# The output biases of three decision trees on TensorE: f32 products over 128 rows, or bf16 products over 32 rows in three exact parts

## What is computed

```python
def _fff(x, node_w, node_b, w1, b1, w2, b2):
    for _ in range(DEPTH):                      # DEPTH = 4
        score = jnp.einsum('nd,nd->n', xf, node_w[cur]) + node_b[cur]
        cur = 2 * cur + 1 + (score >= 0).astype(jnp.int32)
    sel = jax.nn.one_hot(cur - N_NODES, N_LEAVES)
    hidden_all = jax.nn.relu(jnp.einsum('nd,ldh->lnh', xf, w1) + b1[:, None, :])
    hidden = hidden_all * sel.T[:, :, None]
    out = jnp.einsum('lnh,lho->no', hidden, w2) + sel @ b2
q, k, v = _fff(x, *q_weights), _fff(x, *k_weights), _fff(x, *v_weights)
attn = jax.nn.softmax(jnp.einsum('bqd,bkd->bqk', q, k) * scale, axis=-1)
return jnp.einsum('bqk,bkd->bqd', attn, v)
```

## Time and profile before

| what | us |
| --- | --- |
| median of three runs | 1132.84 |
| lowest and highest of the three | 1128.87, 1138.29 |
| span of the profiled execution, first to last instruction | 1131.2 |
| TensorE busy in it | 1003.4 (89%) |
| VectorE busy | 620.1 (55%) |
| ScalarE busy | 533.9 (47%) |
| GpSimd busy | 199.7 (18%) |

### The profile page before, as it was taken

One profiled execution on the slowest core, in us unless ns is written; L12 is line 12 of the kernel. 1 busy time (PEld: TensorE's weight loads), 2 busy tenths in 40 slices (PEclk: granted clock), 3 DMA queues, 4 the chain that ended last, 5 costly groups with the idle time before them and its releaser, 6 DMA issues.

```text
span 1131.2 us, 11557 instructions
## 1 busy us (share of the span) xinstructions
PE 1003.4 (89%) x3694; PEld 435.2 (38%) x3694; DVE 620.1 (55%) x1160; ACT 533.9 (47%) x978; POOL 199.7 (18%) x176
## 2 busy tenths in 40 slices
PE   5799999999799999998877996867778999999896
PEld 2345555454222222332233663322224444444343
DVE  2222323332888878767334435379998544645573
ACT  4232223232367667766732442665665424464540
POOL 9100000000000000000274551256663000000000
PEclk9799999999899999999988997989999999999998
DMA  8630000030011211210012436000000211110032
GB/s 168 203 101 1 1 1 1 1 91 0 22 50 43 71 43 42 61 33 1 6 35 52 121 91 190 6 5 1 0 1 1 94 55 47 46 40 19 5 108 75
DMA packets 67020, 54.70 MB, mean 48 GB/s; under 512 B 18584, under 2 KB 58829, under 8 KB 66868
## 3 DMA queue, kind: packets, MB, share of 16 engines
q1 hardware_dynamic: 64660, 51.26, 16.0%
q0 software_dynamic: 2304, 2.76, 0.8%
HBM read 41.65 MB, written 13.77 MB: 49 GB/s over the span
## 4 chain that ended last, share of the span: by engine, by line
PE 71%; DVE 11%; ACT 6%; issue 6%; POOL 2%; DMA 2%; another core or an unknown queue 1%; DVEq 0%; SPq 0%; POOLq 0%; ACTq 0%
PE psum L692 68%; ACT sb_scr L1654 3%; DVE sb_scr L2338 3%; DVE sb_scr L2687 2%; DVE sb_scr L2696 2%; ACT sb_qstack L1654 1%; ACT psum L1654 1%; PE psum L1265 1%; PE psum L849 1%; POOL sb_qstack L626 1%; PE psum L1247 1%; POOL sb_scr L672 0%; DVE sb_scr L2213 0%; DVE sb_x L2189 0%
## 5 line engine op out<-in xcount | busy, mean ns | idle before, releaser
L1654 ACT ACTIVATE sb_scr<-psum 128x512 f32<-128x512 f32 (+3 forms) x640 | 318.6, 536 | 361.6 <-PE psum L692 305.5
L692 PE MATMUL psum<-sb_h,sb_wide 128*128 128x512 f32 x448 | 210.4, 599 | 0.8 <-ACT sb_scr L1654 0.8
L2338 DVE TENSOR_REDUCE sb_scr<-psum 128x2 f32<-128x1024 f32 x128 | 154.9, 1223 | 46.2 <-PE psum L692 45.5
L692 PE MATMUL psum<-sb_scr,sb_wide 128*128 128x512 f32 x256 | 126.3, 594 | 0.8 <-DVE sb_scr L2742 0.8
L692 PEld LDWEIGHTS psum<-sb_h,sb_wide 128*128 128x128 f32 x448 | 83.5, 193 | 93.1 <-issue 91.4
L692 PE MATMUL psum<-sb_kstack,sb_qstack 96*128 96x512 bf16 x256 | 98.4, 395 | 8.3 <-DVE sb_scr L2338 8.1
L2277 DVE TENSOR_SCALAR sb_scr<-psum,sb_b 128x512 f32<-128x512 f32 x48 | 34.6, 748 | 126.1 <-PE psum L692 126.1
L692 PE MATMUL psum<-sb_qstack,sb_kstack 128*128 128x512 bf16 x256 | 99.3, 394 | 3.9 <-ACT sb_scr L1654 2.8
L672 POOL TENSOR_TENSOR sb_scr<-sb_scr 128x512 f32<-128x512 f32 x64 | 83.0, 1302 | 91.7 <-ACT sb_scr L1654 46.0
L1654 ACT ACTIVATE sb_scr<-psum,sb_b 128x512 f32<-128x512 f32 x48 | 31.2, 684 | 137.1 <-PE psum L692 137.1
L643 POOL COPY sb_wide<-sb_wide 128x512 f32<-128x512 f32 x4 | 2.5, 618 | 511.2 <-ACT sb_scr L1654 511.2
(11 more groups left out here) (274 smaller groups left out, 1291.1 us busy)
## 6 DMA issues: line engine op xcount, KB each, us to landing
sb_scr<-weight_rows SPq DMA_DIRECT2D x32, 256.0 KB
sb_qstack<-q_bounce SPq DMA_DIRECT2D x48, 96.0 KB
sb_kstack<-k_bounce SPq DMA_DIRECT2D x144, 32.0 KB
sb_scr<-pick_rows SPq DMA_DIRECT2D x8, 512.0 KB
expert_in<-sb_scr SPq DMA_DIRECT2D x4, 645.0 KB, 6.5
sb_scr<-expert_in SPq DMA_DIRECT2D x8, 322.5 KB
expert_out<-sb_scr SPq DMA_DIRECT2D x4, 512.0 KB, 4.9
sb_scr<-expert_out SPq DMA_DIRECT2D x8, 256.0 KB, 4.9
```

Source lines behind the costliest of these rows:

```text
L692: return nc.tensor.matmul(out_, w, r, start=start, stop=stop, **kw)
L1654: return nc.scalar.activation(out_, in_, func, **kw)
L2338: v.reduce_max(headmax[:, g % 2, t:t + 2, j], banks, AX.X).then_inc(sem("maxed"), 1)
```

## The change

The table b2 is cut once, on VectorE, into three bf16 parts (`b2_parts`), in chunk 4 of batch 0. `leaf`, which holds only zeros and ones, is written as bf16. The bias products leave `down` and become `add_b2(b)`, which is called once a batch behind `up(b, 6)`. It multiplies, for each of the three parts, only the 32 rows of each tree's own leaves: q on rows 0 to 31 of the array, k on rows 32 to 63, v on rows 64 to 95, all in bf16 and into the same banks 3, 4 and 5 as before.

```diff
+        b2_parts = sb("b2_parts", [P, PARTS, 3, D], BF16)
+        b2_rest = sb("b2_rest", [P, 3, D])
...
-        leaf = view(8832, S)
+        leaf = view(8832, S // 2, BF16)
...
                     if f < 2:
-                        m = mm(bank(3 + f), w2[f][:, c, :], acts, c == 0, False)
+                        m = mm(bank(3 + f), w2[f][:, c, :], acts, c == 0, c == HCH - 1)
                     else:
                         for t in range(TT):
 
                             m = mm(psum[:, 5, t * D:(t + 1) * D], acts[:, t * P:(t + 1) * P], w2[f][:, c, :],
-                                   c == 0 and t == 0, False, skip_group_check=True)
-                    if c < HCH - 1:
-                        continue
-                    if f == 0:
-
-                        pe.wait_ge(sem("path_ready"), 2 * b + 2)
-                    if f < 2:
-                        m = mm(bank(3 + f), b2[:, f, :], leaf, False, True)
-                    else:
-                        for t in range(TT):
-                            m = mm(psum[:, 5, t * D:(t + 1) * D], leaf[:, t * P:(t + 1) * P], b2[:, f, :],
-                                   False, t == TT - 1, skip_group_check=True)
-                    m.then_inc(sem("tree_out"), 1)
+                                   c == 0 and t == 0, c == HCH - 1 and t == TT - 1, skip_group_check=True)
+                    if c == HCH - 1:
+                        m.then_inc(sem("tree_out"), 1)
+
+            def add_b2(b):
+
+                pe.wait_ge(sem("path_ready"), 2 * b + 2)
+                if b == 0:
+                    pe.wait_ge(sem("b2_step"), PARTS + 1)
+                for i in range(PARTS):
+                    for f in range(2):
+                        rr = slice(32 * f, 32 * f + 32)
+                        mm(bank(3 + f), b2_parts[rr, i, f, :], leaf[rr, :], False, False, tile_position=(32 * f, 0))
+                    rr = slice(64, 96)
+                    for t in range(TT):
+                        mm(psum[:, 5, t * D:(t + 1) * D], leaf[rr, t * P:(t + 1) * P], b2_parts[rr, i, 2, :], False, False,
+                           tile_position=(64, 0), skip_group_check=True)
...
                     up(b, c)
+                    if c == HCH - 2:
+                        add_b2(b)
                     beside_trees(b, c)
...
+            def split_b2():
+                step = sem("b2_step")
+                dve.wait_ge(sem("trees_rest"), TREES_REST)
+                v.tensor_copy(b2_parts[:, 0], b2[:]).then_inc(step, 1)
+                dve.wait_ge(step, 1)
+                v.tensor_tensor(b2_rest[:], b2[:], b2_parts[:, 0], ALU.subtract).then_inc(step, 1)
+                dve.wait_ge(step, 2)
+                v.tensor_copy(b2_parts[:, 1], b2_rest[:]).then_inc(step, 1)
+                dve.wait_ge(step, 3)
+                v.tensor_tensor(b2_parts[:, 2], b2_rest[:], b2_parts[:, 1], ALU.subtract).then_inc(step, 1)
...
                     beside_trees(b, c)
+                    if (b, c) == (0, HCH // 2):
+                        split_b2()
```

## The result

The changed kernel takes **1117.86 us**, median of four runs (1114.48 to 1120.12), beside 1133.82 of the kernel before (the three runs shown and one more). The ratio is 0.9862, 95% interval 0.9815 to 0.9909: 15.6 us, and 16.0 between the medians, about twice the 7.6 forecast. Here and further on a ratio is an estimate with its own interval, and not quite the quotient of the two medians, so both are given. The profiled execution took 1120.12 us, its span is 1118.3 at a mean granted clock of 0.957; the one of before had a span of 1131.2 at 0.961.

What follows compares the result with a forecast made beforehand. TensorE was taken to bound the trees' stretch, every microsecond on the chain. 10.4 us removed less 2.9 added gave 7.6 us less (rounded from 1.89 a batch), so 1132.8 - 7.6 = 1125.2 us, range 1119.5 to 1131.5.

Steps and rivals of the forecast that it cites:

- Removed: Bias products of q, k and v in each batch's last chunk go: 2.61 us a batch, 10.4 us in four.
- Added on TensorE: 18 bf16 products a batch behind `up`'s three 32-row products: 0.24 us a part, 0.72 a batch, 2.9 in all.
- both changes of mode: Going onto row tiles and back to the full array is already paid by `up`'s group; bias products cost only their columns.
- The price of 0.11 for going back: After `up`'s three 32-row products, returning to the full array costs 0.11 us of the group's 0.33.
- They lie beside q and k: Within a part, v's four 128-column products, 0.23 us together, run alongside those of q and k, 0.22.
- VectorE's cutting: Casts and subtractions of b2 on VectorE in batch 0: about 1.8 us under 3.3 us of cover, nothing late.
- What becomes late: With TensorE faster, no other engine becomes late; the 7.6 us reach VectorE's softmax of the last batch at 278.72 undiminished.
- The rival of the drained tile: A second turn on a row tile waits until it is empty: gain only 2.5 us, 1130.3 us; chance 0.15.
- The products one by one: Rival: the 18 bias products don't run side by side, 3.9 us a batch, 5 us slower, 1137.8 us; chance 0.03.
- The clock: Rival: work behind the trees shifts against the slow-clock pieces, 3.4 us either way, 1128.6 or 1121.8; chance 0.08.
- The three runs before spread over 9.4 us: Allowance for run spread in the whole time: a median may fall 3 or 4 us off.
- the sum 1132.8 - 7.6: Whole-kernel forecast: median of the kernel before less the net gain in the trees, 1125.2 us.

Runs made afterwards that it cites:

- packed form: Changed kernel with two parts of b2 in one 32-row product, 12 bias products a batch in place of 18: 1127.83 us, ratio 0.9958 to the kernel before.
- padded kernel: Changed kernel with nine bf16 products of a zero table behind each batch's bias products: 1135.72 us, ratio 1.0014 to the kernel before.
- first comparison: The first four runs of the changed kernel, unaltered, against the kernel before: 1117.86 us beside 1133.82, ratio 0.9862.
- first and third chip: Two of three follow-up groups, each on its own chip; changed kernel against the kernel before: ratio 0.9938 on the first, 0.9956 second, 0.9975 third.
- by-tree kernel: Changed kernel with the same 18 products a batch ordered q's three parts, k's three, then v's twelve: 1120.37 us, ratio 0.9931 to the kernel before.

## Why the prediction was wrong in its number and right in its steps

**Removed.** Right. The last chain stretch lost 2.61 us, the very sum of the earlier trace rows, and 12 records; the distance lost 7.76, four times 2.61 - 0.67.

**Added on TensorE.** Right within 0.05 us a batch. Said: 0.72 a batch, 0.24 a part. Measured: 0.67 by the timeline and by the kernel without bias products (226.33 - 223.65 in four batches). A part takes 0.22. The second turn on a row tile costs nothing on top of its columns, so the 0.02 to 0.03 that I had taken over from the column tiles of the earlier trace rows isn't there. That both changes of mode are paid by the group of three is shown by 0.99 against 0.32 and by the packed form's 0.77. The price of 0.11 for going back was too low, which costs the sum nothing, as it is paid in either kernel: the first f32 product behind the row tiles takes 0.10 more on top (0.96 against 0.86 in the padded kernel). "They lie beside q and k", of v's four products, is in the starts.

**VectorE's cutting.** Right: the run with the cutting alone is 1.0011. The four instructions fill 72.13 to 74.07 (1.94 us where 1.8 was said), and the next ReLU still waits 1.49 us for TensorE.

**What becomes late.** Nothing, as said. "4.42 - 2.61 leaves 1.8" is 1.80 in the row above. The gain reached VectorE's softmax whole. That it starts at 271.08 where 271.1 was written is partly luck: the gain in the trees was 0.2 larger than said (7.76), and they began 0.12 later.

**The rival of the drained tile** (parts 0.66 apart) is out: they are 0.22 apart. The rule of the Trainium skill that spoke for it (the page "TensorE: Matmul & The Clock Gate", "Part 3: Packing small matmuls": a weight load overlaps only when it goes to other rows) does not hold in this trace: the loads for the next part go to the very rows that are computing (82.15 beside the products of 82.13), and the part still takes only its columns. The same part of that page makes an exception for a load into the background weight buffer; no run here shows whether that is what happens. **The products one by one** are out as well: a kernel that makes them so, on all rows, needed 0.67 a part, where the changed one needs 0.22. **The clock**, priced at 3.4 us either way, is not out. On one chip the changed kernel's mean clocks were lower, worth 2 to 4 us by the fit, and the gain between medians fell to 5.7 and 4.4 us: under the 6 that the prediction itself had named as a sign of the clock. Whether the change brings that is open, as said above. Of the first comparison it explains a part at most: there the changed kernel's clock was a favourable 0.9598, worth 2.7 us beside 0.957.

**The step that failed** is the last one: "The three runs before spread over 9.4 us, so a median may fall 3 or 4 us off", and with it the sum 1132.8 - 7.6, which carries the median of before over as if after were run under the same conditions. The gain of the change is 7.76 us in the trees, and 4.4 to 7.3 us between medians on one chip (2.8 to 7.0 by the ratios), 8.6 at one clock. In place of a spread of 3 or 4 us the runs showed that the same kernel differs by 6.2 to 7.0 us between chips at one clock. The first comparison's 15.6 us hold some 7 us more than the 8.6. These fit a difference between chips: VectorE's standstill and a long expert phase (119.6 to 124.9 us) are in every profile from the first and third chip, in both kernels, and in none from the second, where the kernel before is 4.6 to 6.4 us faster between medians too. The profiles of the first comparison are one of either kind, and by the fit so are their times. On which chips that comparison ran isn't recorded, though; that its two sides were on chips of different kinds is inferred, not shown. Against it one could hold the fourth run of before, which came with those of after and took 1134.79 us; but runs of before reached 1135.47 on the second chip too, and neither chip nor clock of this one is on record. The term was mis-sized, not the mechanism: a bound of 3 or 4 us taken from three runs has no place in it for a difference of 6 us that those runs, if all on one chip, could not show. With 1128.5 as the value of before, the sum would have been 1120.9. The 3.0 us that are then left are of the size of that comparison's favourable clock (0.9598, beside 0.956 for the kernel before on the second chip).

**What stays open.** Why VectorE waits at this step until GpSimd has ended its scatters on some chips and not on others; the profile names no releaser on the core ("remote"), and nothing in the kernels differs. And the lower mean clock of the changed kernel's runs.

## What to carry to other kernels

Small products whose rows fit beside each other are worth about a third of their price when three of them lie on three row tiles, and the price of going onto the tiles is paid once: put them next to work that is already there, and fill the rows of a tile before adding a turn. Before the total, look at the distance between two fixed points in both timelines, one ahead of the change and one behind it: it gave 7.76 us from one execution of each kernel and repeated within 0.01, while totals on three chips said 4.4, 5.7 and 7.3 between medians, with intervals of 3 to 4 us either side. A single fixed point is not enough: the start of the trees moved by up to 1.4 us from one execution to the next. And compare a kernel only with runs of the other on the same chip, then at the same mean clock; a ratio between chips can hold more than the change.

## What the runs showed of the hardware that I had not expected

- The second and third turn on a 32-row tile cost only their columns: parts 0.22 us apart, the pace of full 512-column bf16 products here (0.216 in the padded kernel's nine), with new weights on the same rows each time.
- Going back from row tiles to the full array costs about 0.2 us, in two pieces: 0.11 until the next product starts, and 0.10 more in that product if it is f32 (0.96 against 0.86).
- Products on different row tiles start together although the program has three to six others between them: v's first product at 81.92 behind six of q and k, in the by-tree kernel.
- One kernel differs by 6 to 7 us of 1130 between chips at the same mean clock (1135.6, 1128.6, 1134.8), and the changed kernel in the same way (1126.7, 1120.2, 1126.2). About 6 us lie in the expert phase (119.6 to 124.9 us in seven profiles on the first and third chip, mean 121.2; 114.5 to 116.4 in four on the second, mean 115.1), where VectorE takes a step 3.1 to 7.1 us late beside GpSimd's indirect DMAs on two chips and under 0.4 late on the other.
- 0.001 of mean granted clock is worth 0.95 us here, and taking it into account brings the scatter of single runs from some 3 to 6 us (a standard deviation) down to 1.8.
